# Delta-rule recurrence: keys times decay from VectorE, negative values and state reads summed in one PSUM bank, one solve

## The chip, the cores and the metric

The program runs on one core of one Trainium2 chip, in FP32 throughout. The metric is the device time of one execution in microseconds (us); the kernel before was timed three times. TensorE is PE in the profile, VectorE is DVE, ScalarE is ACT, GpSimd is POOL, and SyncE, which issues the DMA transfers, is SP.

## The reference

The whole is one pre-norm transformer layer on 8 batches of 512 tokens with width 128: attention by a recurrence, then a mixture of 8 experts. The change is in the recurrence alone:

```python
def step(S, inp):
    q_t, k_t, v_t, b_g, b_beta = inp
    S = S * jnp.exp(b_g)[..., None, None]
    kv = jnp.einsum('mbhk,mbhkv->mbhv', k_t, S)
    dv = (v_t[None] - kv) * b_beta[..., None]
    S = S + k_t[..., :, None] * dv[..., None, :]
    o_t = jnp.einsum('mbhk,mbhkv->mbhv', q_t, S)
    return (S, o_t)
```

There are 8 modes, 8 batches and 8 heads; the state S of each is 64 x 64. Keys and queries are rotated by an angle that depends on the mode, values are shared by the modes of a head. The kernel works in chunks of 64 tokens. Within a chunk the new values W solve a triangular system: W = X (V - K' S), where X is the inverse that holds the products of keys, decays and beta, K' are the keys times the decay from the start of the chunk, and S is the state at the chunk's start. Then S becomes S times the chunk's decay plus the keys (with their decay to the chunk's end) times W, and the outputs are the scores times W plus the decayed queries times S.

## The kernel before

`program` runs `prepare` (projections and tables into DRAM), `recurrence` and `experts`. `recurrence` goes through 64 sequences (8 heads times 8 batches). In step k every engine works on two of them: it *runs* sequence k and *prepares* the next. The 8 modes of a sequence lie as 4 pairs (`PAIRS`), one mode of a pair on partitions 0 to 63 and the other on 64 to 127. A sequence has 8 chunks, c = 0 to 7 (`SUPER` = 8, `SPAN` = 64 tokens, `WRITES` = 7, `NT` = 4 blocks of 128 tokens). A loop goes over the first 7 heads with the 8 steps of a head written out in it, and the last head stands behind it.

Preparing, on VectorE (lines 958 to 972): `rotate(i)` makes rotated keys and queries of a block of 128 tokens in `KP` (L893, L894, L901), `take_scores(c)` multiplies the products of keys with keys and queries from PSUM by the decays into `SC` (L926), `decayed_q(i)` makes `Qd`, the queries times decay (L921), then `to_lanes` (L932), 30 rounds of `eliminate` (L942, L943) and `from_lanes` (L954, L955) invert the 32 x 32 triangles. The next sequence's `rotate(0)` comes right behind. TensorE makes the scores from `KP` (`scores`, L1053 and L1057), the keys by tokens (`token_keys`, L1073), transposes of the next window (`transposes`, L1011), and the 64 x 64 inverses from the 32 x 32 ones (`merge`, L1034 and L1036).

Running, for each chunk c from 1 to 7: TensorE does `solve_values` (inverse `XN` times values `V`, L1094), `read_state` (keys times state, L1082), `outputs` (L1125, L1135), then `solve_reads` (inverse times `R`, L1103, added to the same PSUM region), `keep_state` (L1108, identity times the decayed state `Sdec`) and `write_state` (L1118). ScalarE copies between them: `R` from the read, scaled for each mode pair by a column of `col` (L846, four instructions), `Sdec` (L850, four), `W` from the solve (L853), and `S` from the written state (L859). For c = 0 the state is zero, so that only `solve_values` and `write_state` are left. The work of preparing is laid between these parts in an order written out by hand: `PE_PLACES` and `ACT_PLACES` say how many pieces go before and behind each solve. So TensorE makes scores 0 to 7 beside chunks 0 to 3: score 0 ahead of `solve_values(0)`, score 1 ahead of `write_state(0)`, scores 2 and 3 about the solve of chunk 1, scores 4, 5 and 6 about that of chunk 2, and score 7 ahead of the solve of chunk 3.

For each 64 x 64 product a mode pair needs two matmuls, one for each half of the partitions, and the profile has two MATMUL records for one FP32 matmul: a group of 8 products is x16, and the one full-width product of `keep_state` is x2.

On SP, `load_win`, `load_g` (which waits for all 8 scores to be taken) and `load_eg` are issued in this order in each step. `EG` holds the decays in two slots.

Of the kernel before, what the change touches and what calls it, by code (L numbers as in the profile page):

```python
# [605 lines left out]
def recurrence(nc, sems, fresh, c_mat, ident, KQ_s, V_s, G_s, EG_s, COL_s, TAB_s, O_s):  # L606

    GROUP = SUPER // 2
    with ExitStack() as ctx:
# [7 lines left out]
        KP = sb("KP", [128, 3, PAIRS, T])  # L617
        Qd = sb("Qd", [128, 2, PAIRS, T])

# [8 lines left out]
        decay = sb("decay", [128, 2, PAIRS, SUPER])  # L628
        EG = sb("EG", [128, 2, PAIRS, T])

# [21 lines left out]
        with nc.Block() as block:  # L652
            @block.sync
            def _(sp):
                sp.dma_start(below[:, :], c_mat[3, :, 0:SPAN]).then_inc(l_const, 16)
                sp.wait_ge(l_const, 16)

            @block.vector
            def _(dve):
                for bank in SP + PR:  # L660
                    dve.memset(bank[:, :], 0.0).then_inc(dve_s, 1)
                dve.memset(XN[:, :, :, :], 0.0).then_inc(dve_s, 1)
                for e in range(2):
                    rows = slice(64 * e + C, 64 * e + SPAN)
                    dve.tensor_copy(ZM[rows, :, :, C:], bcast(bcast(ident[rows, rows], 1, SUPER), 1, PAIRS)).then_inc(dve_s, 1)
                dve.wait_ge(dve_s, 8)
        fresh()

        RUNS, WRITES = SUPER, SUPER - 1

        def emit(n0, h0, odd, steps, first=False):
# [17 lines left out]
            with nc.Block() as block:  # L689
                @block.sync  # L690
                def _(sp):
                    def load_win(n):
                        sp.dma_start(win[:, :, :], KQ_s.rearrange("h b p i e -> (h b) p i e")[bass.ds(n, 1)].rearrange("a p i e -> p (a i) e")).then_inc(l_win, 16)

                    def load_eg(n, slot):
                        for e in range(2):
                            sp.dma_start(EG[64 * e:64 * e + 64, slot],
                                         EG_s.rearrange("h b m t -> (h b) m t")[bass.ds(n, 1), e::2, :].broadcast_to([64, PAIRS, T])).then_inc(l_eg, 16)
# [15 lines left out]
                    if first:  # L714
                        load_win(n0 + 1)
                        load_tab(h0, range(4))
                        load_g(n0 + 1)
                        load_eg(n0 + 1, (odd + 1) % 2)
                    ran = prepared = loads = 0
                    for k, (runs, prepares, more) in enumerate(steps):  # L720
                        now, par = parts(k)
                        if prepares:
                            if k:

                                sp.wait_ge(pe_o, RUNS * k)
                            n = n0 + (k + 1)
                            sp.dma_start(col[:, par], COL_s.rearrange("h b p k a c -> (h b) p k a c")[bass.ds(n, 1)].rearrange("a p k b c -> (a p) k b c")).then_inc(l_col, 16)
                            for e in range(2):
                                sp.dma_start(V[64 * e:64 * e + 64, par],
                                             V_s.rearrange("h b t c e -> (h b) t c e")[bass.ds(n, 1)].rearrange("a t c e -> (a t) c e")).then_inc(l_v, 16)  # L730
                            prepared += 1
                        if more:
                            n = n0 + (k + 2)
                            sp.wait_ge(scored, SUPER * k + 2)
                            if k + sets:
                                sp.wait_ge(pe_t, 4 * (k + sets))
                            load_win(n)
                            sp.wait_ge(scored, SUPER * (k + 1))
                            load_g(n)
                            if k == 6:  # L740

                                sp.wait_ge(rot_k, NT * (k + 1))
                                load_tab(h0 + 1, (0, 1))
                                sp.wait_ge(rot_q, NT * (k + 1))
                                load_tab(h0 + 1, (2, 3))
                            if k:
                                sp.wait_ge(qd_done, 5 * k)
                            load_eg(n, now)
                            loads += 1
                        if runs:  # L750

                            sp.wait_ge(act_o, k + 1)
                            sp.dma_start(O_s[bass.ds(n0 + k, 1)].rearrange("a (i p) v -> p (a i) v", p=128), O[:, k % 2]).then_inc(stored, 16)
                            ran += 1
# [12 lines left out]
                def _(act):  # L767
                    token_rows = PR[0][:, :].rearrange("p (z a f) -> p z a f", z=2, a=PAIRS)
                    for k, (runs, prepares, more) in enumerate(steps):
# [67 lines left out]
                        else:  # L837
                            plan = ACT_PLACES if prepares else [1] + [0] * (2 * SUPER - 1)
                            for c in range(SUPER):
                                if c:  # L840
                                    act.wait_ge(pe_r, WRITES * k + c)
                                    if c == 1 and k:
                                        act.wait_ge(l_col, 16 * k)
                                        act.wait_ge(qd_done, 5 * k)
                                    for p in range(PAIRS):
                                        last = act.activation(R[:, p, :], KS[:, 0, p, :], ACT.Copy, scale=col[:, now, 1, p, c:c + 1])  # L846
                                    last.then_inc(act_r, 1)
                                    if c < WRITES:
# [3 lines left out]
                                act.wait_ge(pe_w, RUNS * k + c + 1)  # L852
                                act.copy(W[:, :, :], WP[:, 0]).then_inc(act_w, 1)  # L853
                                for _ in range(plan[2 * c]):
# [17 lines left out]
                def _(dve):  # L872
                    v = Chain(dve, dve_s)
                    for k, (runs, prepares, _) in enumerate(steps):
# [4 lines left out]
                        def products(query, i):  # L879
# [3 lines left out]
                            if i == 0:  # L883
# [4 lines left out]
                                if k:  # L888
                                    dve.wait_ge(pe_o, RUNS * k)
                                    dve.wait_ge(qd_done, 5 * k)  # L890
                                    dve.wait_ge(scored, SUPER * k)
# [22 lines left out]

                        def decayed_q(i):
                            if i == 0:
                                here(dve, l_eg, 2, k)
                                dve.tensor_copy(decay[:, par], EG[:, par, :, SPAN - 1::SPAN]).then_inc(qd_done, 1)
                                dve.wait_ge(rot_q, NT * (k + 1))
                            t = slice(128 * i, 128 * i + 128)  # L920
                            dve.tensor_tensor(Qd[:, par, :, t], EG[:, par, :, t], KP[:, 2, :, t], ALU.mult).then_inc(qd_done, 1)  # L921

# [42 lines left out]
                        for i in range(NT):  # L965
                            decayed_q(i)
                            take_scores(3 + i)
# [23 lines left out]
                def _(pe):  # L991
                    wins = turned = 0
                    token_rows = PR[0][:, :].rearrange("p (z a f) -> p z a f", z=2, a=PAIRS)
                    for k, (runs, prepares, more) in enumerate(steps):
# [66 lines left out]
                        def token_keys(c2):  # L1061
# [12 lines left out]
                            last.then_inc(pe_kd, 1)  # L1074

                        def read_state(c):

                            pe.wait_ge(act_f, WRITES * k + c)
                            for p in range(PAIRS):
                                for e in range(2):  # L1080
                                    f = slice(64 * e, 64 * e + 64)
                                    last = pe.matmul(KS[f, 0, p, :], KP[f, now, p, SPAN * c:SPAN * c + SPAN], S[f, c % 2, p, :], start=True, stop=True)  # L1082
                            last.then_inc(pe_r, 1)

                        def solve_values(c):
# [12 lines left out]
                        def solve_reads(c):  # L1098
                            pe.wait_ge(act_r, WRITES * k + c)
                            for p in range(PAIRS):  # L1100
                                for e in range(2):
                                    f = slice(64 * e, 64 * e + 64)
                                    last = pe.matmul(WP[f, 0, p, :], XN[f, p, c, :], R[f, p, :], start=False, stop=(p == PAIRS - 1))  # L1103
                            last.then_inc(pe_w, 1)
# [22 lines left out]
                        def outputs(c):  # L1127

                            if c == 1 and k:
                                pe.wait_ge(qd_done, 5 * k)  # L1130
                                pe.wait_ge(act_o, k)
# [461 lines left out]
```

## Time and profile before

| What | Value |
|---|---|
| Median of 3 runs | 4784.18 us (4780.45 to 4792.02) |
| Profiled execution | 4793.02 us |
| Its span | 4790.8 us |
| PE, DVE, ACT, POOL busy | 84%, 76%, 61%, 8% of the span |
| Mean granted TensorE clock | 0.873 of full speed |
| `run_O` copies (one for each of 64 sequences) | first at 537.1 us, last at 4314.8 us |

The span is the time from the first to the last instruction in the trace; times in the rows are microseconds from its start. "[idle before <-releaser]" says how long the engine had stood idle before an instruction and what ended it. The granted clock is 1.00 at 2.4 GHz and 0.50 at 1.2 GHz. Most of the time is the recurrence, from about 400 to 4315 us.

### The profile page before, as it was taken

The numbers are of one execution on the slowest core, as the hardware profiler recorded it, in microseconds if no ns is written. First come the engines' busy times: TensorE is split into PE (matmuls) and PEld (weight loads), VectorE is DVE, ScalarE is ACT, GpSimd is POOL, SyncE is SP. The second block draws the span as 40 slices with busy tenths as digits, with TensorE's granted clock in tenths as the row PEclk, the third lists the DMA queues.
The fourth block names the chain that finished last, engine by engine and source line by source line (L and its number), as shares of the span: only waits on it lengthen the run. The fifth ranks groups of instructions, "written<-read, shape, count | busy, mean of one in ns | idle before, by whom it ended". The sixth has DMA issues, their size and how long they took to land. (4 is left out here: it accounts for less than half of the span.)

```text
span 4790.8 us, 195228 instructions
## 1 busy us (share of the span) xinstructions
PE 4015.4 (84%) x85713; PEld 3307.7 (69%) x85713; DVE 3652.5 (76%) x7742; ACT 2902.2 (61%) x9736; POOL 371.3 (8%) x156
## 2 busy tenths in 40 slices
PE   5502999889988998889889988898899889987999
PEld 2201777777777777777777777777777777775666
DVE  6754888778877887788778877887788778854655
ACT  5742666666666666666666666666566666654443
POOL 1221000000000000000000000000000000000000
PEclk8755889889888998899889988998899889988999
DMA  4675222322232223222322231223122312203110
GB/s 119 167 182 133 52 51 56 83 53 52 52 87 53 52 52 87 53 52 52 87 53 52 52 87 47 57 52 87 40 59 58 82 44 58 57 10 83 36 31 7
DMA packets 283082, 314.77 MB, mean 66 GB/s; under 512 B 135768, under 2 KB 182752, under 8 KB 278112
## 3 DMA queue, kind: packets, MB, share of 16 engines
q1 hardware_dynamic: 282208, 301.99, 26.7%
q8 instruction: 687, 11.26, 1.0%
q14 instruction: 187, 1.53, 0.1%
HBM read 232.70 MB, written 69.21 MB: 63 GB/s over the span
## 5 line engine op out<-in xcount | busy, mean ns | idle before, releaser
L926 DVE TENSOR_TENSOR run_SC<-run_SP,run_DB 128x512 f32<-128x512 f32 x512 | 350.1, 687 | 474.6 <-PE run_SP L1057 468.3
L943 DVE TENSOR_TENSOR run_XL<-run_XL,run_EL 128x30 f32<-128x30 f32 (+14 forms) x1920 | 637.3, 332 | 66.0
L942 DVE TENSOR_TENSOR run_EL<-run_AL,run_XL 128x30 f32<-128x30 f32 (+14 forms) x1920 | 636.7, 332 | 66.0
L1053 PE MATMUL run_SP<-run_KP 64*32 64x128 f32 x8192 | 624.8, 302 | 24.5 <-DVE run_KP L901 12.7
L980 POOL TENSOR_TENSOR run_DB<-run_DB,run_below 128x2048 f32<-128x2048 f32 x64 | 297.9, 4655 | 3613.7 <-DVE run_XL L943 3487.9
L801 ACT ACTIVATE run_DB<-run_DB,run_col 128x64 f32<-128x64 f32 x2048 | 537.3, 337 | 12.0 <-POOL run_DB L980 4.2
L1053 PEld LDWEIGHTS run_SP<-run_KP 64*32 64x32 f32 x8192 | 465.6, 119 | 101.8 <-issue 50.0
L859 ACT COPY run_S<-run_KS 128x256 f32<-128x256 f32 x448 | 166.9, 373 | 556.5 <-PE run_KS L1118 556.5
L808 ACT ACTIVATE run_KD<-run_PR,run_col 128x64 f32<-128x64 f32 x2048 | 471.6, 327 | 12.9 <-PE run_PR L1073 6.8
L846 ACT ACTIVATE run_R<-run_KS,run_col 128x64 f32<-128x64 f32 x1792 | 416.0, 323 | 102.8 <-PE run_KS L1082 102.4
L1057 PE MATMUL run_SP<-run_KP 64*32 64x64 f32 x8192 | 454.5, 243 | 0.0
L1036 PE MATMUL run_PR<-run_XO,run_ZM 32*64 32x32 f32 x8192 | 422.9, 275 | 36.9 <-ACT run_ZM L778 36.6
L893 DVE TENSOR_TENSOR run_tmpv<-run_tab,run_kqT 128x512 f32<-128x512 f32 x512 | 372.2, 727 | 104.7 <-ACT run_kqT L793 37.6
L1011 PE MATMUL run_PR<-ident,run_win 128*64 128x128 f32 x4096 | 299.8, 283 | 178.0 <-DMA run_win<-KQ_s 154.0
L1036 PEld LDWEIGHTS run_PR<-run_XO,run_ZM 32*64 32x64 f32 x8192 | 406.1, 202 | 50.6 <-ACT run_ZM L778 41.5
L850 ACT ACTIVATE run_Sdec<-run_S,run_decay 128x64 f32<-128x64 f32 x1536 | 413.5, 364 | 0.0
L1094 PE MATMUL run_WP<-run_V,run_XN 64*64 64x64 f32 x8192 | 375.9, 237 | 39.9 <-issue 39.1
L1011 PEld LDWEIGHTS run_PR<-ident,run_win 128*64 128x64 f32 x4096 | 238.9, 141 | 208.7 <-DMA run_win<-KQ_s 154.3
L1073 PE MATMUL run_PR<-ident,run_KP 64*64 64x64 f32 x8192 | 294.1, 221 | 92.8 <-ACT run_KD L808 90.8
L1094 PEld LDWEIGHTS run_WP<-run_V,run_XN 64*64 64x64 f32 x8192 | 325.0, 152 | 65.9 <-issue 65.9
L1073 PEld LDWEIGHTS run_PR<-ident,run_KP 64*64 64x64 f32 x8192 | 260.8, 134 | 146.5 <-issue 142.2
L1125 PE MATMUL run_OB<-run_W,run_SC 128*64 128x64 f32 x4096 | 361.5, 234 | 0.5 <-ACT run_W L853 0.5
(201 smaller groups left out, 7588.8 us busy)
## 6 DMA issues: line engine op xcount, KB each, us to landing
run_DB<-G_s SPq DMA_DIRECT2D x256, 256.0 KB
run_EG<-EG_s SPq DMA_DIRECT2D x128, 512.0 KB, 8.9
run_tab<-TAB_s SPq DMA_DIRECT2D x128, 256.0 KB, 10.5
KQ_s<-proj_win SPq DMA_DIRECT2D x32, 768.0 KB, 7.8
run_win<-KQ_s SPq DMA_DIRECT2D x64, 384.0 KB, 3.1
TAB_s<-tab_tab SPq DMA_DIRECT2D x128, 128.0 KB, 2.4
run_V<-V_s SPq DMA_DIRECT2D x128, 128.0 KB, 2.6
V_s<-proj_vv SPq DMA_DIRECT2D x64, 128.0 KB, 3.1
```

The source lines that it names most:

```text
L801: last = act.activation(DB[:, p, c, :], DB[:, p, c, :], ACT.Exp, bias=col[:, par, 0, p, c:c + 1])
L808: last = act.activation(KD[:, par, p, c, :], token_rows[:, c % 2, p, :], ACT.Copy, scale=col[:, par, 2, p, c:c + 1])
L846: last = act.activation(R[:, p, :], KS[:, 0, p, :], ACT.Copy, scale=col[:, now, 1, p, c:c + 1])
L850: last = act.activation(Sdec[:, p, :], S[:, c % 2, p, :], ACT.Copy, scale=decay[:, now, p, c:c + 1])
L942: v.link(dve.tensor_tensor(e, bcast(AL[:, r + 1:, r], 2, done), bcast(XL[:, r, 0:done], 1, rows), ALU.mult))
L943: less = dve.tensor_tensor(XL[:, r + 1:, 0:done], XL[:, r + 1:, 0:done], e, ALU.subtract)
L1011: last = pe.matmul(PR[1][64 * e:64 * e + 64, 128 * i:128 * i + 128], win[:, i, off:off + DK], ident[:, :], start=True, stop=True)
L1036: last = pe.matmul(to[64 * e:64 * e + SPAN], ZM[two, p, c, :], XO[two, p, c, :], start=True, stop=True)
L1053: pe.matmul(out[64 * e:64 * e + C, p].rearrange("p (z u) i -> p z (u i)", z=2), KP[f, par, p, t0:t1], KP[f, kq, p, t0:t0 + SPAN], start=Tr ...
L1057: last = pe.matmul(out[64 * e + C:64 * e + SPAN, p, 0::3, :], KP[f, par, p, t1:t1 + C], KP[f, kq, p, t1:t1 + C], start=True, stop=True)
L1073: last = pe.matmul(token_rows[f, z, p, :], KP[f, par, p, t0:t0 + SPAN], ident[f, f], start=True, stop=True)
L1094: last = pe.matmul(WP[f, 0, p, :], XN[f, p, c, :], V[f, now, c, :], start=(p == 0), stop=(c == 0 and p == PAIRS - 1))
```

## The change

Four things change. VectorE makes `Kd`, the keys times decay, beside `Qd` (four more multiplications of 128 x 512 for each sequence). `solve_values(c)` goes for c > 0; in its place one full-width product of a negative identity with `V`, repeated over the pairs (`less_values`), puts -V into the second half of bank `WP`, and `read_state` adds `Kd` times S on top of it. The copy into `R` is one plain copy in place of four scaled ones. `solve` is then one set of products for each chunk, and the copy into `W` multiplies by -1 for c > 0. `EG` has one slot in place of two, and `load_eg` waits for the products of its own step.

```diff
-        Qd = sb("Qd", [128, 2, PAIRS, T])
+        Qd, Kd = sb("Qd", [128, 2, PAIRS, T]), sb("Kd", [128, 2, PAIRS, T])
...
-        EG = sb("EG", [128, 2, PAIRS, T])
+        EG = sb("EG", [128, PAIRS, T])
+        nident = sb("nident", [128, 128])
...
+                dve.tensor_scalar(nident[:, :], ident[:, :], -1.0, None, ALU.mult).then_inc(dve_s, 1)
...
-        RUNS, WRITES = SUPER, SUPER - 1
+        RUNS, WRITES, DECAYED = SUPER, SUPER - 1, 1 + 2 * NT
...
-                            if k:
-                                sp.wait_ge(qd_done, 5 * k)
-                            load_eg(n, now)
+                            sp.wait_ge(qd_done, DECAYED * (k + 1))
+                            load_eg(n)
...
-                                    for p in range(PAIRS):
-                                        last = act.activation(R[:, p, :], KS[:, 0, p, :], ACT.Copy, scale=col[:, now, 1, p, c:c + 1])
-                                    last.then_inc(act_r, 1)
+                                    act.copy(R[:, :, :], WP[:, 1]).then_inc(act_r, 1)
...
-                                act.copy(W[:, :, :], WP[:, 0]).then_inc(act_w, 1)
+                                if c == 0:
+                                    act.copy(W[:, :, :], WP[:, 0]).then_inc(act_w, 1)
+                                else:
+                                    act.activation(W[:, :, :], WP[:, 0], ACT.Copy, scale=-1.0).then_inc(act_w, 1)
...
-                        def decayed_q(i):
+                        def decayed(i):
                             if i == 0:
                                 here(dve, l_eg, 2, k)
-                                dve.tensor_copy(decay[:, par], EG[:, par, :, SPAN - 1::SPAN]).then_inc(qd_done, 1)
+                                dve.tensor_copy(decay[:, par], EG[:, :, SPAN - 1::SPAN]).then_inc(qd_done, 1)
+                                dve.wait_ge(rot_k, NT * (k + 1))
                                 dve.wait_ge(rot_q, NT * (k + 1))
                             t = slice(128 * i, 128 * i + 128)
-                            dve.tensor_tensor(Qd[:, par, :, t], EG[:, par, :, t], KP[:, 2, :, t], ALU.mult).then_inc(qd_done, 1)
+                            dve.tensor_tensor(Qd[:, par, :, t], EG[:, :, t], KP[:, 2, :, t], ALU.mult).then_inc(qd_done, 1)
+                            dve.tensor_tensor(Kd[:, par, :, t], EG[:, :, t], KP[:, par, :, t], ALU.mult).then_inc(qd_done, 1)
...
+                        def less_values(c):
+
+                            if c == 1 and k:
+                                pe.wait_ge(qd_done, DECAYED * k)
+                            pe.matmul(WP[:, 1], nident[:, :], bcast(V[:, now, c, :], 1, PAIRS), start=True, stop=False)
+
...
-                                    last = pe.matmul(KS[f, 0, p, :], KP[f, now, p, SPAN * c:SPAN * c + SPAN], S[f, c % 2, p, :], start=True, stop=True)
+                                    last = pe.matmul(WP[f, 1, p, :], Kd[f, now, p, SPAN * c:SPAN * c + SPAN], S[f, c % 2, p, :], start=False, stop=(p == PAIRS - 1))
...
-                        def solve_values(c):
+                        def solve(c):
...
+                            if c:
+                                pe.wait_ge(act_r, WRITES * k + c)
...
-                                    last = pe.matmul(WP[f, 0, p, :], XN[f, p, c, :], V[f, now, c, :], start=(p == 0), stop=(c == 0 and p == PAIRS - 1))
-                            if c == 0:
-                                last.then_inc(pe_w, 1)
-
-                        def solve_reads(c):
...
-                                    last = pe.matmul(WP[f, 0, p, :], XN[f, p, c, :], R[f, p, :], start=False, stop=(p == PAIRS - 1))
+                                    last = pe.matmul(WP[f, 0, p, :], XN[f, p, c, :], R[f, p, :] if c else V[f, now, c, :], start=(p == 0), stop=(p == PAIRS - 1))
                             last.then_inc(pe_w, 1)
...
                                 if c:
-                                    solve_values(c)
+                                    less_values(c)
                                     read_state(c)
                                     outputs(c)
...
-                                if c == 0:
-                                    solve_values(c)
-                                else:
-                                    solve_reads(c)
-                                    if c < WRITES:
-                                        keep_state(c)
+                                solve(c)
+                                if 0 < c < WRITES:
+                                    keep_state(c)
```

The other waits for `qd_done` count 9 for each step (`DECAYED`) in place of 5.

## Rows read from the trace of the kernel before

**Rows 1.** The page, busy time of each engine over the whole span.

```profile
PE 4015.4 (84%) x85713; PEld 3307.7 (69%) x85713; DVE 3652.5 (76%) x7742; ACT 2902.2 (61%) x9736; POOL 371.3 (8%) x156
```

**Rows 2.** DVE timeline of one sequence: start, duration, line, shapes, idle before.

```profile
1517.02 1.22 DVE L893 TENSOR_TENSOR run_tmpv<-run_tab,run_kqT 128x512 f32<-128x512 f32 x1
...
1533.91 0.68 DVE L921 TENSOR_TENSOR run_Qd<-run_EG,run_KP 128x512 f32<-128x512 f32 x1
1534.51 0.68 DVE L926 TENSOR_TENSOR run_SC<-run_SP,run_DB 128x512 f32<-128x512 f32 x1
...
1537.25 0.69 DVE L926 TENSOR_TENSOR run_SC<-run_SP,run_DB 128x512 f32<-128x512 f32 x1 [1.47 <-PE run_SP L1057]
...
1540.36 0.69 DVE L926 TENSOR_TENSOR run_SC<-run_SP,run_DB 128x512 f32<-128x512 f32 x1 [0.62 <-PE run_SP L1057]
1543.73 0.69 DVE L926 TENSOR_TENSOR run_SC<-run_SP,run_DB 128x512 f32<-128x512 f32 x1 [2.68 <-PE run_SP L1057]
...
1573.22 1.23 DVE L893 TENSOR_TENSOR run_tmpv<-run_tab,run_kqT 128x512 f32<-128x512 f32 x1
```

**Rows 3.** Waits from 480 to 4315 us: total us, times, longest.

```profile
DVE run_SC L926 <- PE run_SP L1057: 468.3, 300, 5.7
...
DVE run_tmpv L893 <- ACT run_kqT L793: 37.6, 7, 6.2
...
PE run_WP L1103 <- ACT run_R L846: 33.8, 71, 0.5
```

**Rows 4.** Windows: length, busy PE, PEld, DVE, ACT, POOL, granted PE clock, DMA.

```profile
478.00:4211.00 3733.00, 3330.18 (x80684) 2851.16 (x80686) 3050.89 (x6325) 2400.64 (x8804) 282.55 (x63) 0.89 0.26 60
```

**Rows 5.** Windows: two neighbouring sequences, and a stretch of each.

```profile
1517.00:1573.20 56.20, 50.98 (x1304) 43.46 (x1300) 49.13 (x102) 38.64 (x142) 4.54 (x2) 0.94 0.24 56
1573.20:1633.10 59.90, 53.87 (x1229) 45.99 (x1227) 49.51 (x102) 38.75 (x142) 4.61 (x2) 0.86 0.21 48
...
1525.20:1544.50 19.30, 19.28 (x533) 16.33 (x534) 14.50 (x26) 13.36 (x52) 0.00 (x0) 1.00 0.08 25
1573.20:1590.00 16.80, 16.00 (x297) 14.48 (x294) 15.26 (x25) 9.60 (x27) 0.70 (x1) 0.50 0.08 24
```

**Rows 6.** PE timeline about chunk 1 of the first of them, clock 1.00.

```profile
1528.10 0.68 PE L1118 MATMUL run_KS<-run_W,run_KD 64*64 64x64 f32 x16
1528.61 0.63 PE L1094 MATMUL run_WP<-run_V,run_XN 64*64 64x64 f32 x16
1529.25 0.68 PE L1082 MATMUL run_KS<-run_S,run_KP 64*64 64x64 f32 x16
...
1531.47 0.68 PE L1103 MATMUL run_WP<-run_R,run_XN 64*64 64x64 f32 x16
1532.10 0.70 PE L1108 MATMUL run_KS<-run_Sdec,ident 128*128 128x256 f32 x2
1532.73 0.30 PE L1053 MATMUL run_SP<-run_KP 64*32 64x128 f32 x2
```

**Rows 7.** ACT timeline about the same chunk.

```profile
1528.83 0.37 ACT L859 COPY run_S<-run_KS 128x256 f32<-128x256 f32 x1 [1.02 <-PE run_KS L1118]
```

**Rows 8.** PE timeline about chunk 1 of the second sequence, clock 0.50.

```profile
1586.66 1.12 PE L1118 MATMUL run_KS<-run_W,run_KD 64*64 64x64 f32 x16
1587.56 1.06 PE L1094 MATMUL run_WP<-run_V,run_XN 64*64 64x64 f32 x16
1588.42 1.06 PE L1082 MATMUL run_KS<-run_S,run_KP 64*64 64x64 f32 x16
1589.41 0.37 PE L1125 MATMUL run_OB<-run_W,run_SC 128*64 128x64 f32 x1
```

**Rows 9.** One group from 480 to 4315 us: count, busy, mean ns, idle before.

```profile
L778 ACT ACTIVATE run_ZM<-run_PR 128x512 f32<-128x512 f32 x128 | 75.7, 592 | 29.0 <-PE run_PR L1034 27.3
```

**Rows 10.** ACT timeline of the last sequence, where nothing is prepared beside it.

```profile
4303.01 0.93 ACT L846 ACTIVATE run_R<-run_KS,run_col 128x64 f32<-128x64 f32 x4 [0.84 <-PE run_KS L1082]
...
4307.50 0.93 ACT L846 ACTIVATE run_R<-run_KS,run_col 128x64 f32<-128x64 f32 x4 [0.84 <-PE run_KS L1082]
```

More of the change, by code:

```diff
@@ L665, in _ @@
                     dve.tensor_copy(ZM[rows, :, :, C:], bcast(bcast(ident[rows, rows], 1, SUPER), 1, PAIRS)).then_inc(dve_s, 1)
-                dve.wait_ge(dve_s, 8)
+                dve.wait_ge(dve_s, 9)
         fresh()
-        RUNS, WRITES = SUPER, SUPER - 1
+        RUNS, WRITES, DECAYED = SUPER, SUPER - 1, 1 + 2 * NT
         def emit(n0, h0, odd, steps, first=False):
@@ L693, in load_win, with load_eg @@
                         sp.dma_start(win[:, :, :], KQ_s.rearrange("h b p i e -> (h b) p i e")[bass.ds(n, 1)].rearrange("a p i e -> p (a i) e")).then_inc(l_win, 16)
-                    def load_eg(n, slot):
+                    def load_eg(n):
                         for e in range(2):
-                            sp.dma_start(EG[64 * e:64 * e + 64, slot],
+                            sp.dma_start(EG[64 * e:64 * e + 64],
                                          EG_s.rearrange("h b m t -> (h b) m t")[bass.ds(n, 1), e::2, :].broadcast_to([64, PAIRS, T])).then_inc(l_eg, 16)
@@ L717, in _ @@
                         load_g(n0 + 1)
-                        load_eg(n0 + 1, (odd + 1) % 2)
+                        load_eg(n0 + 1)
                     ran = prepared = loads = 0
@@ L843, in _ @@
                                         act.wait_ge(l_col, 16 * k)
-                                        act.wait_ge(qd_done, 5 * k)
-                                    for p in range(PAIRS):
-                                        last = act.activation(R[:, p, :], KS[:, 0, p, :], ACT.Copy, scale=col[:, now, 1, p, c:c + 1])
-                                    last.then_inc(act_r, 1)
+                                        act.wait_ge(qd_done, DECAYED * k)
+                                    act.copy(R[:, :, :], WP[:, 1]).then_inc(act_r, 1)
                                     if c < WRITES:
@@ L889, in products @@
                                     dve.wait_ge(pe_o, RUNS * k)
-                                    dve.wait_ge(qd_done, 5 * k)
+                                    dve.wait_ge(qd_done, DECAYED * k)
                                     dve.wait_ge(scored, SUPER * k)
@@ L965, in _ @@
                         for i in range(NT):
-                            decayed_q(i)
+                            decayed(i)
                             take_scores(3 + i)
@@ L1093, in solve_values @@
                                     f = slice(64 * e, 64 * e + 64)
-                                    last = pe.matmul(WP[f, 0, p, :], XN[f, p, c, :], V[f, now, c, :], start=(p == 0), stop=(c == 0 and p == PAIRS - 1))
-                            if c == 0:
-                                last.then_inc(pe_w, 1)
-                        def solve_reads(c):
[L1099 to L1102, printed above, removed]
-                                    last = pe.matmul(WP[f, 0, p, :], XN[f, p, c, :], R[f, p, :], start=False, stop=(p == PAIRS - 1))
+                                    last = pe.matmul(WP[f, 0, p, :], XN[f, p, c, :], R[f, p, :] if c else V[f, now, c, :], start=(p == 0), stop=(p == PAIRS - 1))
                             last.then_inc(pe_w, 1)
@@ L1129, in outputs @@
                             if c == 1 and k:
-                                pe.wait_ge(qd_done, 5 * k)
+                                pe.wait_ge(qd_done, DECAYED * k)
                                 pe.wait_ge(act_o, k)
```

## The prediction

> **What bounds the kernel now.** I read the page first. No engine is full over the span: PE 84%, DVE 76%, ACT 61% [rows 1]. So something alternates, and the question is which engine holds the loop over the 64 sequences at each place. I took the DVE timeline of one sequence next, because DVE ends a sequence with a chain of its own and starts the next behind it. From the first rotation at 1517.02 to the next at 1573.22 are 56.2 us [rows 2]. Behind the last score, taken at 1543.73, there is not one wait up to the next rotation: 29.5 us of DVE work back to back (transposes and elimination). Ahead of it DVE stands idle three times, for 1.47, 0.62 and 2.68 us, and each time what ends it is PE's scores [rows 2]. Over the recurrence these waits are 468.3 us in 300 pieces, by far the largest of DVE's [rows 3]. The loop is therefore: DVE rotates, PE makes scores 0 to 7 between pieces of the running sequence, and when score 7 is there DVE has a fixed 29.5 us left. PE in that stretch is full: 19.28 of 19.30 us busy at clock 1.00, and 16.00 of 16.80 at clock 0.50 [rows 5]. So a microsecond that PE gains or loses ahead of score 7 moves the end; one that PE or ACT gains behind it does not, unless something else is late.
>
> The windows show a second thing: neighbouring sequences differ. The first is 56.20 us at mean clock 0.94, the next 59.90 at 0.86, and nearly all of the second's first 16.8 us ran at 0.50 [rows 5]. PE's work is the same; the clock makes the 3.7 us. The mean clock over 3733 us is 0.89 [rows 4], which is between 0.94 and 0.86 at 5/8 of the way, so about 5 sequences in 8 are like the slow one. I call the two kinds F and S.
>
> **The change part by part.** *Four Kd products on DVE.* The row of the same shape is Qd, 0.68 us with the next instruction 0.60 behind it [rows 2]; four are 2.4 us for a sequence. One stands ahead of each of the takes 3 to 6. Take 3 comes at 1535.1 in place of 1534.5; take 4 had 1.47 idle and absorbs the two products ahead of it (1.2); take 5 comes 0.6 late, and take 6, which had 0.62 idle, has again two ahead of it and comes about 0.6 late, ending near 1541.6; take 7 is due at 1543.73. So of its 2.68 idle some 2.1 stay and the products are hidden by waits for PE. Nothing that PE needs gets late: score 6 needs the buffer of take 3 (free at 1535.7, used behind 1539), score 7 that of take 4, which doesn't move. Cost 0. With the cover gone it is 2.4 x 63 = 151 us. Only the very first preparation has no running sequence beside it; there 2.4 us can show once.
>
> *R and W on ACT.* Four scaled instructions of 128 x 64 (0.93 us for the four) [rows 10] become one plain copy of 128 x 256; the copy of S has that shape and takes 0.37 [rows 7]. That saves 0.56 us for a chunk. The scale of -1 on W costs nothing: a copy scaled by -1 over 128 x 512 takes 592 ns [rows 9], less than two plain ones of half its width (0.37 each) [rows 7]. But what waits for R? PE waited for it 33.8 us in all, 71 times among 448 [rows 3], and in the stretch with the scores PE has filler behind the read (outputs and a score: read at 1529.25, solve at 1531.47) [rows 6]. So the 0.56 is worth 0 in 62 sequences. In the last one nothing is prepared beside it and a chunk takes 4.49 us from R to R, with R on the chain [rows 10]: there it is worth about 0.46 (0.56 less the 0.1 below), for 7 chunks 3 us. ACT gets no new work.
>
> *PE.* For chunks 1 to 7, 8 products of 64 x 64 (x16) go and one of 128 x 128 by 128 x 256 (x2) comes. PE loses 98 of its 1304 matmul records of a sequence, 7.5%. That looks like a large gain, and it is none: the one wide product is as long as the eight. Its twin is keep_state, same shapes: it starts at 1532.10 and the next group at 1532.73, 0.63 us [rows 6]. solve_values starts at 1528.61, read_state at 1529.25, 0.64 [rows 6]. Moreover the 0.64 is not all work: the read needs the S copy, which ends at 1528.83 + 0.37 = 1529.20 [rows 7]. From write_state's start to the read are 1.15 us, set by that copy. Now add the entry: where a wide product follows a group of eight (solve_reads, then keep_state) the group's pitch is 0.63 [rows 6], where a group of eight follows write_state it is 1528.61 - 1528.10 = 0.51. With less_values in that place the sum is 0.63 + 0.63 = 1.26 against 1.15: +0.11 for a chunk at clock 1.00. Bounds: 0 (if entry costs nothing: 0.51 + 0.63 is just under the 1.15 of the copy) and +0.11. I take +0.11 since its row shows the same pair of shapes.
> The page TensorEngine Tiling of the Trainium skill, section Key Properties, says that a change of tiling mode drains TensorE. By that rule the change is to be feared, as it adds two changes of mode in each chunk. The 0.12 between 0.63 and 0.51 agrees with it on the way in; on the way out no separate price is seen, for it lies within the 0.63.
>
> At clock 0.50 the groups are 0.90 (write_state), 0.86 (solve_values), and 0.99 for a group of eight followed by a wider shape (read, then outputs) [rows 8]. The wide product never ran at that clock. Between 0.86 (no longer than what it replaces) and 2 x 0.63 = 1.26 (all of it goes by the clock) I take 1.26, because it is two long passes and not many short ones. Then 0.99 + 1.26 = 2.25 against 1.76: +0.49, with bounds +0.13 and +0.49.
> The Trainium skill, TensorE: Matmul & The Clock Gate, section "Wait — 56ns, not 53.3ns?", gives a long matmul as its columns over the clock and hence twice the time at half of it; the sum by it would be the same 1.26, and no row of this case shows it.
>
> Three chunks lie ahead of score 7 (1, 2 and 3). Kind F has all three at 1.00: +0.33. Kind S has chunk 1 at 0.50 (its 0.50 stretch ends near 1590, behind the values at 1587.56 [rows 5, 8]): +0.49 + 0.22 = +0.71. With 5 in 8 of kind S: 0.375 x 0.33 + 0.625 x 0.71 = 0.57 for a sequence, x 63 = +36 us. Bounds: 0 for F and 0.13 for S give +5; the top is this same +36.
>
> *Waits.* less_values(1) waits for Qd and Kd of a sequence prepared a step ago, done long before. The solve's wait for R is the old one. load_eg now waits for all 9 products of its own step, but stands on SP behind load_g, which already waits for take 7, and the products lie ahead of take 7 on DVE. So nothing is queued behind a new wait, and the single slot of EG is refilled where it was before. Cost 0.
>
> *Where PE's chain is late.* Once for each head DVE waits for the last transposed window, 37.6 us in 7 times [rows 3]: there PE itself stands without instructions while tables come in. With 7.5% fewer matmul records this may ease: from 0 to 16 us (7 x 2.3, taking the second idle of some 2.7 as the size of one such stall), I take 7.5% of 37.6 = 3.
>
> Sum: +36 (PE) - 3 (last sequence) - 3 (once for each head) = +30. The profiled execution is 4790.8 of span and 2.2 about it, 4793.02; it gives 4823. It lies 8.8 above the median of the runs, so the forecast against these is 4784 + 30 = 4814 us, +0.6%. What a measurement of this kernel can tell from no change is about 0.3%, or 14 us.
>
> **The rivals.** *Hidden.* The wide product costs at half clock no more than the group, and its entry fits under the S copy: +5 - 6 = about 4784. For it speaks that the copy alone sets the 1.15 with 0.12 of play; against it the 0.63 of solve_reads ahead of keep_state [rows 6].
>
> *Faster by the clock.* What sets whether a sequence is F or S is what PE does before and at its start: PE waits there for DVE's transposes and then works on small merges. The change alters the last chunks (R comes sooner, +0.11 for the wide product) and so where that idle time falls. Each sequence that turns from S to F is worth 59.9 - 56.2 = 3.7 us. From 12 of the 39 or so on the change is faster than before by over 0.3% (30 - 12 x 3.7 = -14); with 16 it would be 4755. Nothing in the rows tells the direction: the same mechanism with 15 sequences turned from F to S gives 4870, and I count that case with the forecast, since it has the same sign.
>
> *DVE becomes the bound.* If take 7 finds score 7 ready, the Kd products show: 0.3 us for a sequence beyond the 2.1 of play would be +19, all of it +151 (4935). Against it speak the 2.68 idle just there and that PE gets later, not sooner.
>
> *A shorter chain shows everywhere.* Were ACT's 0.56 on the path of chunks 1 to 3, it would be 3 x 0.56 x 63 = 106 us less, 4708 with the other terms. PE busy 19.28 of 19.30 in that stretch speaks against it; I give it little.
>
> **How the numbers follow.** Forecast, with its side of more S sequences: 0.5. Hidden: 0.25. Faster by the clock 0.15, shorter chain 0.05, DVE bound 0.05. Faster by over 0.3%: 0.20; within 0.3%: 0.26; slower: 0.54. The range goes from 4755 (16 sequences turned to F) to 4870 (15 turned to S); outside it lie the shorter chain, the DVE bound and the far ends of the clock's mix.
>
> **What would show it.** In the profile after: L1118's group ahead of the wide product 0.63 long and the wide one 0.63, read_state 1.26 behind write_state's start in place of 1.15, and about 2.25 at clock 0.50; DVE's idle ahead of take 7 near 2.4 in kind F and of take 6 gone; 29.5 us from take 7 to the next rotation unchanged; R as one instruction of 0.37; the last sequence's chunk about 4.0 long. The forecast is wrong if the read comes 1.15 behind write_state, if the mean granted clock over the recurrence moves from 0.89 by more than 0.01, or if ACT's saved time shows between two rotations.

## The result and the profile after

The change makes the kernel slower. Four runs have a median of 4829.74 us (4821.02 to 4838.87), against 4782.32 us before (four runs as well); the ratio is 1.0095, with a 95% interval from 1.0069 to 1.0121. The forecast was 4814 us, +0.6%, in a range of 4755 to 4870.

The page of the changed kernel, its span and the busy time of each engine:

```profile
span 4836.6 us, 181725 instructions
...
PE 4100.3 (85%) x79441; PEld 3261.5 (67%) x79441; DVE 3800.1 (79%) x7999; ACT 2661.1 (55%) x8392; POOL 370.7 (8%) x156
```

PE has 6272 matmul records fewer than before (7.3%) and is busy 85 us longer [rows 1]. ACT has lost 241 us of busy time, and the time of the kernel has not fallen with it.

How long a sequence takes can be read from the first and the last start of the transpose that ends the preparation of each (64 of them, 63 steps between). The kernel before, then the changed one:

```profile
L955 DVE STREAM_TRANSPOSE run_XO<-run_XL x64: 1881/1936/1999, 476.3 to 4269.4; 128x1024 f32<-128x1024 f32 x64
```

```profile
L960 DVE STREAM_TRANSPOSE run_XO<-run_XL x64: 1892/1939/2006, 477.6 to 4316.7; 128x1024 f32<-128x1024 f32 x64
```

That is 3793.1 / 63 = 60.21 us before and 3839.1 / 63 = 60.94 after: 0.73 us for a sequence, 46.0 in all, and the two spans differ by 45.8. All of the loss is in this loop over the sequences.

PE's timeline about chunk 2 of a sequence at clock 1.00, and about chunk 1 of the next at 0.50 (write_state, the new wide product, the read):

```profile
1600.36 0.68 PE L1122 MATMUL run_KS<-run_W,run_KD 64*64 64x64 f32 x16
1600.97 0.70 PE L1085 MATMUL run_WP<-run_V,run_nident 128*128 128x256 f32 x2
1601.60 0.68 PE L1093 MATMUL run_WP<-run_S,run_Kd 64*64 64x64 f32 x16
...
1653.54 1.12 PE L1122 MATMUL run_KS<-run_W,run_KD 64*64 64x64 f32 x16
1654.59 1.22 PE L1085 MATMUL run_WP<-run_V,run_nident 128*128 128x256 f32 x2
1655.74 1.08 PE L1093 MATMUL run_WP<-run_S,run_Kd 64*64 64x64 f32 x16
```

At 1.00 the group of write_state has become 0.61 long (0.51 before), the wide product is 0.63, and the read starts 1.24 us behind write_state's start in place of 1.15 [rows 6]: +0.09. At 0.50 it is 1.05 + 1.15 = 2.20 in place of 1.76 [rows 8]: +0.44.

DVE's timeline about the takes 4 to 7 of the same sequence, with the new products (L926) between them:

```profile
1603.97 0.69 DVE L931 TENSOR_TENSOR run_SC<-run_SP,run_DB 128x512 f32<-128x512 f32 x1 [1.57 <-PE run_SP L1062]
...
1605.18 0.69 DVE L926 TENSOR_TENSOR run_Kd<-run_EG,run_KP 128x512 f32<-128x512 f32 x1
...
1607.58 0.68 DVE L931 TENSOR_TENSOR run_SC<-run_SP,run_DB 128x512 f32<-128x512 f32 x1
1610.54 0.69 DVE L931 TENSOR_TENSOR run_SC<-run_SP,run_DB 128x512 f32<-128x512 f32 x1 [2.27 <-PE run_SP L1062]
...
1640.11 1.22 DVE L896 TENSOR_TENSOR run_tmpv<-run_tab,run_kqT 128x512 f32<-128x512 f32 x1
```

Take 6 (1607.58) no longer waits, take 7 still waits 2.27 us for PE, where it waited 2.68 [rows 2]. From take 7 to the next rotation are 29.6 us, as before (29.5). So DVE is not what holds up take 7.

Windows: the whole loop, then two neighbouring sequences, then one of the short kind:

```profile
480.00:4319.00 3839.00, 3464.62 (x75742) 2848.81 (x75744) 3246.04 (x6678) 2200.51 (x7620) 282.83 (x63) 0.87 0.25 58
1580.80:1640.10 59.30, 54.32 (x1199) 44.72 (x1194) 51.67 (x106) 34.98 (x121) 4.59 (x2) 0.88 0.22 52
1640.10:1700.30 60.20, 55.79 (x1225) 45.83 (x1222) 51.75 (x106) 34.99 (x121) 4.54 (x2) 0.86 0.22 52
2560.20:2616.60 56.40, 51.14 (x1100) 41.76 (x1094) 51.55 (x106) 34.33 (x120) 4.63 (x2) 0.91 0.22 49
```

The mean clock of the loop has gone from 0.89 [rows 4] to 0.87 (with one digit more, 0.886 and 0.871). A sequence of kind F takes 56.40 us (56.20 before) and one of kind S 60.20 (59.90) [rows 5]; these are single sequences. But the neighbours are now an S of 60.20 and one of 59.30, which was a rarer kind between the two before. I counted the sequences with no more than 10.3 us at clock 0.50 between their start and take 7: 22 of 63 before, 6 after (5 or 7 if a sequence is taken to start a little earlier or later). The time at 0.50 between first rotation and take 7, summed over the 63 sequences, is 804 us before and 907 after. So there are two parts: the kinds themselves got longer, by up to 0.3 us, and the mix of kinds got worse.

Against it stands one gain. DVE's waits at a sequence's start, for the last transposed window, in the kernel before and then in the changed one:

```profile
DVE run_tmpv L893 <- issue: 37.3, 6, 7.0
```

```profile
DVE run_tmpv L896 <- issue: 29.0, 6, 5.1
DVE run_tmpv L896 <- ACT run_kqT L795: 27.7, 12, 5.0
```

The wait that ACT ended was 37.6 [rows 3] and is 27.7, the one put down to "issue" was 37.3 and is 29.0: together 18 us less.

### The profile page after: what moved, and what is told of

It is laid out like the page before. It is cut to its first block and busy times, and to the rows that moved or that the text cites. A ratio compares the mean times of both kernels' runs of the same rounds, so it can differ in the third digit from the quotient of the medians.

```text
span 4836.6 us, 181725 instructions
## 1 busy us (share of the span) xinstructions
PE 4100.3 (85%) x79441; PEld 3261.5 (67%) x79441; DVE 3800.1 (79%) x7999; ACT 2661.1 (55%) x8392; POOL 370.7 (8%) x156
## 5 line engine op out<-in xcount | busy, mean ns | idle before, releaser
L1058 PE MATMUL run_SP<-run_KP 64*32 64x128 f32 x8192 | 635.5, 306 | 23.9 <-DVE run_KP L904 12.7
L1041 PE MATMUL run_PR<-run_XO,run_ZM 32*64 32x32 f32 x8192 | 445.5, 282 | 44.6 <-ACT run_ZM L780 36.7
L1041 PEld LDWEIGHTS run_PR<-run_XO,run_ZM 32*64 32x64 f32 x8192 | 427.4, 211 | 59.6 <-ACT run_ZM L780 41.8
L856 ACT ACTIVATE run_W<-run_WP 128x256 f32<-128x256 f32 x448 | 171.5, 383 | 447.6 <-PE run_WP L1107 447.6
L1129 PE MATMUL run_OB<-run_W,run_SC 128*64 128x64 f32 x4096 | 355.0, 230 | 30.1 <-issue 29.6
L1093 PEld LDWEIGHTS run_WP<-run_S,run_Kd 64*64 64x64 f32 x7168 | 257.6, 140 | 171.0 <-ACT run_S L862 159.9
L897 DVE TENSOR_TENSOR run_KP<-run_tab,run_kqT 128x512 f32<-128x512 f32 x512 | 348.7, 681 | 0.0
```

Source lines behind the costliest of these rows:

```text
L1041: last = pe.matmul(to[64 * e:64 * e + SPAN], ZM[two, p, c, :], XO[two, p, c, :], start=True, stop=True)
L1058: pe.matmul(out[64 * e:64 * e + C, p].rearrange("p (z u) i -> p z (u i)", z=2), KP[f, par, p, t0:t1], KP[f, kq, p, t0:t0 + SPAN], start=Tr ...
L1129: return pe.matmul(place(c), SC[:, 1 + now, p, c, :], W[:, p, :], start=(c == 0 and p == 0), stop=(p == PAIRS - 1))
```

## The experiments

All were timed in rounds with the kernel before on the same chip. "Short sequences" are those of 63 with at most 10.3 us at clock 0.50 ahead of take 7, counted in the one profiled run of each (22 before), and uncertain by one or two.

| Run | Ratio to before | 95% interval | Short sequences |
|---|---|---|---|
| the change | 1.0095 | 1.0069 to 1.0121 | 6 |
| e1_narrow | 1.0008 | 0.9993 to 1.0023 | 24 |
| e2_wide_only | 1.0135 | 1.0111 to 1.0158 | 9 |
| e3_kd_only | 1.0004 | 0.9988 to 1.0019 | 29 |
| e4_plain_r | 1.0001 | 0.9985 to 1.0018 | 27 |
| e5_wide_early | 1.0096 | 1.0069 to 1.0122 | 18 |
| e6_wide_late | 0.9963 | 0.9942 to 0.9984 | 25 |
| e7_dve_delay | 1.0049 | 1.0032 to 1.0067 | 12 |
| e8_reorder | 0.9968 | 0.9951 to 0.9985 | 29 |
| e9_late_reorder | 0.9978 | 0.9960 to 0.9995 | 29 |
| e10_reorder_wide | 1.0124 | 1.0108 to 1.0139 | 8 |

**Which part of the change costs the time?** First the whole change with the one wide product made narrow.

```diff
-                            pe.matmul(WP[:, 1], nident[:, :], bcast(V[:, now, c, :], 1, PAIRS), start=True, stop=False)
+                            for p in range(PAIRS):
+                                for e in range(2):
+                                    f = slice(64 * e, 64 * e + 64)
+                                    pe.matmul(WP[f, 1, p, :], nident[f, f], V[f, now, c, :], start=(p == 0), stop=False)
```

> The whole change, but the negative values go into the bank by 8 products of 64 x 64 (x16) in place of one wide product (x2); everything else of the change stays. If the wide product is the cause, the slowdown of 0.95% goes: between write_state's start and the read 1.15 us again, 1.76 at clock 0.50, and a time of 4770 to 4790 us (ratio 0.997 to 1.002), with some 20 sequences again of the kind whose slow-clock stretch is 6.8 us. If VectorE's four products or the shorter R copy are the cause, it stays near 4828 (ratio 1.008 to 1.011).

Measured: 4792.69 us against 4785.63, 1.0008. The loss is gone. Its PE timeline about a chunk at 1.00 is the one of before, 0.51 and 0.64:

```profile
1523.30 0.68 PE L1125 MATMUL run_KS<-run_W,run_KD 64*64 64x64 f32 x16
1523.81 0.63 PE L1088 MATMUL run_WP<-run_V,run_nident 64*64 64x64 f32 x16
1524.45 0.68 PE L1096 MATMUL run_WP<-run_S,run_Kd 64*64 64x64 f32 x16
```

Then each part alone in the kernel before. The wide product:

```diff
                         def solve_values(c):
...
+                            if c:
+                                pe.matmul(WP[:, 0], ident[:, :], bcast(V[:, now, c, :], 1, PAIRS), start=True, stop=False)
+                                return
                             for p in range(PAIRS):
```

> The kernel before with one thing of the change: in chunks 1 to 7 the 8 products of inverse and values are replaced by one wide product of the identity with the values into the same region (the inverse is thus left out of this term, so that the output is another). No Kd, R scaled as before, W as before. If the wide product is the cause: 4825 to 4845 us (ratio 1.009 to 1.013), the group of write_state 0.61 and the wide product 0.63 in the trace, and fewer sequences with the short slow-clock stretch. If it is not: 4782.

Measured: 4848.15 us, 1.0135, at least what the whole change costs (1.0095; the two intervals overlap from 1.011 to 1.012). The trace has the same two lengths, 0.61 and 0.63:

```profile
1526.30 0.68 PE L1121 MATMUL run_KS<-run_W,run_KD 64*64 64x64 f32 x16
1526.91 0.70 PE L1092 MATMUL run_WP<-run_V,ident 128*128 128x256 f32 x2
1527.54 0.68 PE L1082 MATMUL run_KS<-run_S,run_KP 64*64 64x64 f32 x16
```

VectorE's four products:

```diff
+                            dve.tensor_tensor(Kd[:, :, t], EG[:, par, :, t], KP[:, par, :, t], ALU.mult).then_inc(qd_done, 1)
```

> The kernel before with VectorE's four Kd products added and nothing reading them. If they are hidden by the waits for the scores: 4782 to 4787 us (ratio 1.000 to 1.001), the wait ahead of take 7 some 2.1 us in place of 2.7. If they are part of the slowdown: up to 0.6 us in each sequence, 4800 to 4820 (ratio 1.004 to 1.008).

Measured: 4783.23 us, 1.0004. The products are there and cost nothing. DVE's waits in this run:

```profile
DVE run_SC L928 <- PE run_SP L1059: 306.2, 224, 5.8
```

They were 468.3 [rows 3]; 162 us of waiting have become some 151 us of products.

The plain copy into R:

```diff
-                                    for p in range(PAIRS):
-                                        last = act.activation(R[:, p, :], KS[:, 0, p, :], ACT.Copy, scale=col[:, now, 1, p, c:c + 1])
-                                    last.then_inc(act_r, 1)
+                                    act.copy(R[:, :, :], KS[:, 0]).then_inc(act_r, 1)
```

> The kernel before with R made by one plain copy of 128 x 256 in place of four scaled ones (the scale by beta and decay is left out). By my steps PE doesn't wait for R ahead of score 7, so 4776 to 4782 us (ratio 0.999 to 1.000): 3 us in the last sequence, something in the sequences where DVE waits for the transposed window. If a shorter chain moves the slow-clock stretches, it shows here as a time off by more than 0.3%, up or down.

Measured: 4786.07 us, 1.0001. ACT is 0.56 us for each chunk shorter and the time does not move. Where nothing lies beside the chain it shows, here from R to R in the last sequence, 3.94 us where it was 4.49 [rows 10]:

```profile
4272.50 0.37 ACT L845 COPY run_R<-run_KS 128x256 f32<-128x256 f32 x1 [0.84 <-PE run_KS L1080]
...
4276.44 0.37 ACT L845 COPY run_R<-run_KS 128x256 f32<-128x256 f32 x1 [0.84 <-PE run_KS L1080]
```

**Does the place count?** The changed kernel with the wide product in only some of the chunks, and the 8 narrow ones in the others.

```diff
+                            if c <= 3:
                                 pe.matmul(WP[:, 1], nident[:, :], bcast(V[:, now, c, :], 1, PAIRS), start=True, stop=False)
+                                return
+                            for p in range(PAIRS):
...
```

> The changed kernel with the wide product only in chunks 1 to 3, which lie ahead of score 7, and 8 narrow products in chunks 4 to 7. If only what PE does ahead of score 7 counts, this is the changed kernel's time, 4820 to 4840 us (ratio 1.007 to 1.012). If the price is the wide product anywhere (7 of them), it is 3 parts in 7 of the loss: about 4805 (ratio 1.004).

Measured: 4837.31 us, 1.0096, the whole loss with 3 of the 7 wide products. But it is made up otherwise than in the changed kernel: there are still 18 short sequences, and the time at 0.50 ahead of take 7 is 815 us (804 before, 907 with the whole change), while the loop is 50 us longer. So the loss of this size doesn't need the worse mix. The other way round, `if c >= 4`:

> The changed kernel with the wide product only in chunks 4 to 7, behind score 7. If only what lies ahead of score 7 counts: 4780 to 4795 us (ratio 0.999 to 1.002), as with narrow products throughout. If the price is the wide product anywhere, 4 parts in 7 of the loss: about 4812 (ratio 1.006). If what moves the slow-clock stretches is the work at the end of a sequence, it shows here as well, with fewer of the short stretches.

Measured: 4768.41 us against 4787.61, 0.9963, faster than before and than e1_narrow (1.0008). The two runs differ from each other in nothing but whether 3 wide products stand ahead of score 7 or 4 behind it, and by 1.3%. Ahead of score 7 PE's time sets the period; behind it there is room. What e6_wide_late has won over e1_narrow stands in one wait: DVE's for the last transposed window is 35.8 us here and 54.7 in e1_narrow, and the two loops differ by 19 us.

```profile
DVE run_tmpv L896 <- ACT run_kqT L795: 35.8, 11, 6.0
```

```profile
DVE run_tmpv L896 <- ACT run_kqT L795: 54.7, 19, 5.4
```

The first line is e6_wide_late's, the second e1_narrow's. That the smaller number of instructions makes it is not shown: the kernel before has as many matmul records as e1_narrow and waits 37.6 [rows 3], and e5_wide_early has 2688 fewer and waits 59.8.

**Is the mix of kinds a mere echo of a longer sequence?** One small DVE instruction more, where DVE waits for nobody:

```diff
                             v.link(dve.memset(XL[:, :, :].rearrange("p i j -> p (i j)")[:, ::C + 1], 1.0))
+                            flat = AL[:, :, :].rearrange("p i j -> p (i j)")
+                            v.link(dve.tensor_tensor(EL[:, 0:108], flat[:, 0:108], flat[:, 108:216], ALU.mult))
```

> The kernel before with one more DVE instruction of 128 x 108 (0.27 us, 0.31 with its link) behind take 7, in the part in which DVE waits for nobody; its result is overwritten. Nothing on PE changes. If a sequence simply gets 0.31 longer: 0.31 x 63 = 20 us, 4805 (ratio 1.004). If a small lengthening also turns sequences from the short slow-clock stretch to a longer one, as in the changed kernel, it is more: 4820 to 4845 (ratio 1.007 to 1.012), with fewer than 22 sequences at 6.8 or 10.2 us of slow clock.

Measured: 4812.49 us, 1.0049, which is 23 us with an interval of 15 to 32. The fixed part of a sequence grew by 0.28 us in the trace, 18 us for 63. So 0.28 us cost about what they are; an echo of up to 14 us is not excluded. The mix did move: the count of short sequences fell to 12 and the time at 0.50 ahead of take 7 rose from 804 to 860 us in the profiled run, about half as much as in the changed kernel. That run, with 4824 us, is the second slowest of its eleven, but the mean clock of all eleven is 0.869 too, against 0.873 for the kernel before beside them. So a longer sequence alone moves the mix in part; an echo that costs as much as in the changed kernel is not seen.

**Can PE's time ahead of score 7 be cut?** In the kernel before PE waits for the S copy ahead of each read. Three scores were moved from ahead of write_state to behind it:

```diff
-                                for _ in range(plan[2 * c + 1]):
+                                later = 1 if prepares and c < 3 else 0
+                                for _ in range(plan[2 * c + 1] - later):
                                     if jobs:
                                         jobs.pop(0)()
                                 pe.wait_ge(act_w, RUNS * k + c + 1)
                                 if c < WRITES:
                                     write_state(c)
+                                for _ in range(later):
+                                    jobs.pop(0)()
```

> The kernel before in another order on PE: scores 1, 3 and 6, which stood ahead of write_state of chunks 0, 1 and 2, come behind it. Then the S copy has a score and the values beside it and PE no longer waits for it ahead of the read (0.17 us in each of chunks 1 to 3 at clock 1.00), while the W copy still lies under keep_state. If PE's time ahead of score 7 sets the period: 0.5 us less for a sequence, 30 us, 4755 (ratio 0.994), more or less by what the slow-clock stretches do (4730 to 4785). If the chain through W is in fact longer than keep_state, PE now waits for it there and the time is the same or up to 40 us more.

Measured: 4771.62 us, 0.9968, a gain of about half of what I expected. The values are now 0.51 long up to the read, where they were 0.64 [rows 6], so the wait for the S copy is gone; write_state, now followed by a score of another shape, is 0.61 in the trace (0.51 before), and that gives most of it back at clock 1.00. What makes up the measured 15 us was not taken apart.

```profile
1519.02 0.68 PE L1118 MATMUL run_KS<-run_W,run_KD 64*64 64x64 f32 x16
1519.63 0.30 PE L1053 MATMUL run_SP<-run_KP 64*32 64x128 f32 x2
...
1520.63 0.68 PE L1094 MATMUL run_WP<-run_V,run_XN 64*64 64x64 f32 x16
1521.14 0.63 PE L1082 MATMUL run_KS<-run_S,run_KP 64*64 64x64 f32 x16
```

Last, this order together with the best version so far, and with the change as it is:

> The changed kernel with the wide product only in chunks 4 to 7 (ratio 0.9963 by itself) and with scores 1, 3 and 6 behind write_state (0.9968 by itself on the kernel before). If the two gains are of different places, one at the end of a sequence and one ahead of score 7, they add up: ratio 0.992 to 0.995, 4750 to 4765 us. If both only shift the slow-clock stretches, the sum is no better than either: 0.996 to 0.998.

Measured: 4765.91 us against 4777.91, 0.9978. The gains don't add up; the three intervals (0.9942 to 0.9984, 0.9951 to 0.9985, 0.9960 to 0.9995) overlap, so that none is shown to be the best, and each is faster than before.

> The changed kernel, wide product in all chunks, with scores 1, 3 and 6 behind write_state. The wait for the S copy then has the score beside it, and the wide product is paid in full: 0.08 longer than the group at clock 1.00 by its length and its entry. If the loss comes from PE's work ahead of score 7, most of it stays: ratio 1.004 to 1.009. If it came from the order in which the read waits for the wide product, it goes: 0.997 to 1.002.

Measured: 4833.71 us, 1.0124, above the 1.009 that I had given as the top. With this order the read has no S copy to wait for and the wide product is as dear as before (0.63 and 1.15, where the eight narrow ones of e8_reorder take 0.51 at clock 1.00); this order, at least, doesn't hide the loss.

## Why the prediction was right

The total and its sign were right, and so was the place of the loss. The size came near by luck: two terms of the sum were off in opposite directions.

**What sets the period: shown.** DVE's fixed stretch behind take 7 did not move (29.6 against 29.5 us), and ACT's shorter copies (e4_plain_r: 1.0001) and DVE's four products (e3_kd_only: 1.0004) are worth nothing. Three wide products ahead of score 7 cost 1.3% more than four behind it (e5_wide_early against e6_wide_late).

**The price of the wide product: the mechanism right, the sizes a little high.** At clock 1.00 I took +0.11 and it is +0.09; at 0.50 I took 1.26 for the product, twice its 0.63, and +0.49 for the chunk, and they are 1.15 (1.8 times) and +0.44. The entry was seen on both sides: 0.61 in place of 0.51. Alone in the kernel before, the wide product makes the whole loss or more (e2_wide_only), and without it the loss is gone (e1_narrow).

**The step that failed is the sum for a sequence.** I gave +0.33 for kind F and +0.71 for kind S; the rows have +0.20 (56.40 against 56.20) and +0.30 (60.20 against 59.90). For kind S one reason is in the windows: the stretch at 0.50 was 16.8 us from the sequence's start before [rows 5] and is 16.5 now, so a little more work runs at full clock. At 0.2 to 0.3 us for 63 sequences the direct part is 13 to 19 us and not 36. These are single sequences; the medians of those that have no wait at their start, away from a change of head, are 56.34 and 56.39 for F, 59.21 and 59.26 for the kind of 59.3, and 59.90 and 60.23 for S, which would make it still less. A second reckoning gives more: what the mix and the start waits below leave over of the 46 us is about 20 us, 0.3 for a sequence. Either way 36 was too high for this kernel.

**The mix of kinds was a term that I had left at 0**, with 3.7 us for each sequence turned and up to 15 of them in the range. In the changed kernel it is the larger part: some 16 sequences fewer are short (22 to 6), and mostly became the kind of 59.3, about 3.1 us longer: 16 x 3.1 = 50 us. The time at 0.50 ahead of take 7 gives nearly the same: it is 103 us longer, and a group that takes 0.90 at 0.50 takes 0.51 at 1.00, so a microsecond at 0.50 costs some 0.43, in all an estimated 44 us. Together with the direct part of 13 to 19 the 50 make 63 to 69; the waits at a sequence's start gave 18 back, for which I had taken 3, and 45 to 51 stand against the measured 46. My own list of signs had the forecast wrong if the mean clock over the recurrence moved from 0.89 by more than 0.01. It moved by 0.015, so by that sign the sum had missed this term, though the total had not.

That the mix moved is counted in the trace. What moves it is not shown. In the changed kernel, e2_wide_only and e10_reorder_wide, which have all seven wide products, there are 6 to 9 short sequences; in the six other kernels that leave DVE's fixed part alone and have none ahead of score 7 there are 24 to 29. But e5_wide_early has the wide product in all the chunks ahead of score 7, still has 18, and loses as much: its 11 us more at 0.50 ahead of take 7 explain some 5 of its 50 us, longer waits at a sequence's start (15 us more, the two kinds of wait shown above together) another 15, and I put the remaining 30 or so down to PE's direct time, which is argued and not shown. So that the wide product ahead of score 7 costs the 1% is shown; how the loss divides between direct time, mix and start waits changes from kernel to kernel. e7_dve_delay shows that a longer sequence by itself moves the mix in part and does not cost that much. One profiled run stands behind each count, so the counts are rough. Why the clock falls or rises at another place stays open.

**The last sequence: right.** From R to R it is 4.04 us in the changed kernel (I said about 4.0), 0.45 less than before:

```profile
4337.01 0.37 ACT L847 COPY run_R<-run_WP 128x256 f32<-128x256 f32 x1 [0.92 <-PE run_WP L1093]
...
4341.05 0.37 ACT L847 COPY run_R<-run_WP 128x256 f32<-128x256 f32 x1 [0.92 <-PE run_WP L1093]
```

**The rivals.** "Hidden" fell with the 1.24 us between write_state and the read. "DVE becomes the bound" and "a shorter chain shows everywhere" fell with e3_kd_only and e4_plain_r. "Faster by the clock" was right in that the mix moves, and had the wrong sign.

So the total came near because errors of opposite sign met: a direct part too high by some 15 to 20 us and a mix that I had at 0 and that cost 44 to 50, less 15 more from the waits at the start.

## What to carry to other kernels

Don't count instructions when small products are to be gathered into a wide one; count the time up to the next group's start, the change of shape on the way in included, and at both clock levels. Then ask on which side of the hand-over to the other engine it lies: the same kind of edit was worth -0.4% behind it (four chunks) and +1% ahead of it (three chunks). And when neighbouring rounds of a loop differ by a clock's stretch, price the change for each kind of round, and keep the number of rounds of each kind as a term of its own, for it can be larger than the direct cost, as in the changed kernel, or small at the same total, as in e5_wide_early.

## What the runs showed of the hardware

- A wide FP32 product (two records of 128 x 256 with full-width weights) took 0.63 us from start to the next group at clock 1.00 and 1.15 at 0.50, 1.8 times as long; eight products of 64 x 64 took 0.51 and 0.90 (write_state's group [rows 6, 8]), also 1.8 times.
- A group of eight 64 x 64 products is 0.10 us longer (0.61 against 0.51) at clock 1.00 and 0.14 (medians over the loop, 1.05 against 0.91) at 0.50 when the next product has another shape, be it full-width (the change) or 64 x 32 (e8_reorder). The Trainium skill says in TensorEngine Tiling, section Key Properties, that a change of tiling mode drains TensorE. The trace agrees in that the group before such a change is longer, by these amounts; that a drain is the reason is not shown.
- DVE's wait for the last transposed window was 35.8 us in e6_wide_late and 54.7 in e1_narrow, which has 7168 more PE instructions (matmuls and weight loads) in the whole program. It doesn't follow the number of instructions throughout: 37.6 in the kernel before, which has as many as e1_narrow, and 32.6 in e3_kd_only, which has as many too.
